# Wide mixing and moved routing products in layer 2, and a new order of all queues for the first two tiles, in a four-layer kernel on one core

## What is computed

```python
# layer 0: conditioning is a grouped convolution plus a bias per batch; ffn is base + LoRA of the best 2 of 28 experts
out = conv(x, weight) + (cond @ c_weight.T)[:, :, None] + bias[None, :, None]
y = out @ base_W.T + lora(out, top2(out @ gate_W.T))
# layers 1, 2, 3: conditioning mixes the 32 channels by a 32x32 table of each batch
h = gelu(gelu(cond @ W0 + b0) @ W1 + b1)
att = softmax(h @ W2 + b2)                                  # 64 x 8
agg_w = einsum('bk,koi->boi', att, weight)                   # 64 tables of 32 x 32
out = einsum('boi,bih->boh', agg_w, x) + (att @ bias_k)[:, :, None]
# ffn of layer 1: an 8-bit fake-quantised 512x512 product
# ffn of layer 2: (silu(out @ W_gate.T) * (out @ W_up.T)) @ W_down.T, 1792 hidden units
# ffn of layer 3: 2 of 3 experts for each batch, chosen by a router that looks at the first row's logits
#   and at the mean |out| of the first 9 channels and of the other 23
```

## Time and profile before

| | us |
|---|---|
| median of 3 runs | 780.34 |
| lowest, highest | 779.86, 783.27 |
| the profiled execution's own time | 779.9 |
| its span in the trace | 778.0 |
| PE busy | 750.6 (96%) |
| DVE, ACT, POOL busy | 478.1 (61%), 275.6 (35%), 419.5 (54%) |
| mean granted clock | 0.985 |

### The profile page before, as it was taken

How to read it: one execution, slowest core, us unless ns; L and a number is a source line. 1 busy time by engine, 2 the same in 40 slices (tenths; PEclk the granted TensorE clock), 3 DMA queues, 4 the chain that set the end, 5 groups by cost and what they waited for, 6 DMA issues and landing times.

```text
span 778.0 us, 11186 instructions
## 1 busy us (share of the span) xinstructions
PE 750.6 (96%) x3644; PEld 605.1 (78%) x3660; DVE 478.1 (61%) x1039; ACT 275.6 (35%) x532; POOL 419.5 (54%) x449
## 2 busy tenths in 40 slices
PE   8999999999899999999999999899899978999997
PEld 5587788787688888888788888777688766888886
DVE  2467667778623255753477256874788888576643
ACT  6444444453432233332424243232342332333211
POOL 2756667775425432111411045778677866778870
PEclk9699999999999999999999999999999998999999
DMA  9446446544051013100331022314313211212110
GB/s 281 71 109 168 160 154 199 164 136 136 28 190 54 28 59 91 55 29 1 94 109 20 10 73 81 131 56 135 124 42 117 60 41 56 69 42 83 55 41 27
DMA packets 49335, 69.60 MB, mean 89 GB/s; under 512 B 25864, under 2 KB 26120, under 8 KB 49016
## 3 DMA queue, kind: packets, MB, share of 16 engines
q1 hardware_dynamic: 39520, 38.65, 16.7%
q0 software_dynamic: 9152, 29.69, 12.5%
q10 hardware_dynamic: 608, 0.55, 0.2%
HBM read 45.71 MB, written 17.66 MB: 81 GB/s over the span
## 4 chain that ended last, share of the span: by engine, by line
PE 79%; DVE 14%; issue 3%; ACT 3%; DVEq 1%; ACTq 0%
PE bank L2024 23%; PE bank L1881 10%; PE bank L1975 9%; PE bank L2007 8%; PE bank L1720 8%; PE bank L1654 4%; PE bank L1758 3%; PE bank L1851 2%; DVE junk L1363 2%; PE bank L1790 1%; PE bank L1986 1%; PE bank L1770 1%; PE bank L1901 1%; DVE tl L1319 1%; ACT th L957 1%
## 5 line engine op out<-in xcount | busy, mean ns | idle before, releaser
L1512 DVE TENSOR_TENSOR sil<-bank,sil 128x512 f32<-128x512 f32 x56 | 38.6, 690 | 95.2 <-PE bank L2024 95.2
L1975 PE MATMUL bank<-wda,xch 128*128 (+1 forms) x272 | 87.9, 405 | 4.3 <-DVE xcl L1537 4.3
L2024 PE MATMUL bank<-th,wgr 128*128 128x512 f32 x224 | 88.3, 394 | 2.5 <-POOL tl L563 1.8
L1881 PE MATMUL bank<-wda,hh 128*128 128x512 f32 x224 | 88.4, 394 | 0.0
L2024 PE MATMUL bank<-th,wur 128*128 128x512 f32 x224 | 87.4, 390 | 0.0
L1881 PE MATMUL bank<-wda,hl 128*128 128x512 f32 x224 | 87.3, 390 | 0.0
L2024 PE MATMUL bank<-tl,wgr 128*128 128x512 f32 x224 | 87.2, 389 | 0.0
L2024 PE MATMUL bank<-tl,wur 128*128 128x512 f32 x224 | 87.2, 389 | 0.0
L1060 ACT ACTIVATE hh<-sil 128x512 fp32r<-128x512 f32 x56 | 35.4, 632 | 109.4 <-DVE sil L1512 109.4
L790 POOL TENSOR_TENSOR raw<-raw,bias 128x512 f32<-128x512 f32 x48 | 67.1, 1397 | 4.0
L1514 DVE TENSOR_TENSOR hl<-sil,hh 128x512 fp32r<-128x512 f32 x56 | 44.7, 798 | 39.1 <-ACT hh L1060 39.1
(11 more groups left out here) (329 smaller groups left out, 1880.4 us busy)
## 6 DMA issues: line engine op xcount, KB each, us to landing
tap<-in_x_taps_dram SPq DMA_DIRECT2D x16, 260.0 KB, 3.0
xin<-in_x_rows_dram SPq DMA_DIRECT2D x16, 256.0 KB, 3.0
xd<-xo SPq DMA_DIRECT2D x16, 256.0 KB, 3.2
xc<-xd SPq DMA_DIRECT2D x16, 256.0 KB, 3.3
xres<-xd SPq DMA_DIRECT2D x4, 1024.0 KB, 5.5
xd<-xres SPq DMA_DIRECT2D x4, 1024.0 KB, 4.7
tsd<-tf SPq DMA_DIRECT2D x4, 1024.0 KB
raw<-in_w_dram POOLq DMA_DIRECT2D x16, 256.0 KB, 3.1
```

What stands on the lines that cost most here:

```text
L1512: v.tensor_tensor(hf[:, m % 2], p_pre[(2 * m + 1) % 3][:], sil[:, m % 2], ALU.mult).then_inc(s_hf, 1)
L1881: last = mm(p_acc[j][:], h[:, m % HSLOTS, j * P:(j + 1) * P], wda[:, m * D:(m + 1) * D], start=(m == 0 and n == 0), stop=(m == MT - 1 and ...
L1975: last = mm(bank[(p + 1) % 2][:], x, y, start=(k == 0 and n == 0), stop=(k == KT - 1 and n == 2))
L2024: last = mm(p_pre[(2 * m + b) % 3][:], w[:, (m * KT + kt) * P:(m * KT + kt + 1) * P], x[:, kt], start=(kt == 0 and n == 0), stop=(kt == KT ...
```

## The change

**Tables.** The mix tables and biases come as one array of 64 x (3, 132), go through high and low parts (`mixh` on POOL, `mixl` on DVE), and three DMAs on POOL's queue (`stack_rows`) lay high, low and high rows over each other, 24 rows (`mix3`). `att3` holds the attention's high, high and low part side by side, 24 columns. `mixed(l)` is then one product with 24 rows for each of three banks, 396, 396 and 264 columns of split float32, with the bias in it.

**First two tiles.** PE: base(0) directly after conv(1), waiting for each quarter of the low weights; mixing_weights and mixed(0) after hidden(0), ahead of lora(0); mixed(1) after router(1); mixed(2) after conv(2); mix1(0) ahead of weights_t. POOL takes over `w0l`, DVE the second half of the weights' rounding (`weight_integers`). On POOL diag_tile(0), tap_lo(3) and diag_lo(0) follow each other. DVE does the softmax after gating(0) and `weight_scales` after t0_lo(1). ACT's order follows these.

**Boundaries of layer 2.** For groups 1 to 3 `cond2(c, j)` mixes tile j by three products of 512 columns ahead of down2 in m = 10..13, ACT adds the bias (`rows2_out`) into `tf`, and `features_t` transposes it with 16 float32 transposes between the groups; `t_hi_p` (ACT) and `t_lo_p` (DVE) take `th` and `tl` from PSUM. POOL's `t_lo`, DVE's `t_rows` and the bias broadcast stay for group 0 alone. x_hi and x_lo of tiles 2 and 3 move into m = 10..12.

**Routing products.** router_sums, class_rows, ranks(0) and permutation(0) stand behind down2(s, m-2) of their slice.

```diff
+            pool.wait_ge(d_mix, 16)
+            nc.gpsimd.tensor_scalar(mixh[:], mixr[:], 1.0, 1.0, ALU.mult, ALU.mult).then_inc(s_mix, 1)
+            pool.wait_ge(s_mix, 1)
+            stack_rows(0, mixh[:])
+            stack_rows(2, mixh[:])
+            pool.wait_ge(s_mix, 2)
+            stack_rows(1, mixl[:])
             tap_lo(1)
+            for k in range(KT):
+                pool.wait_ge(s_w0s, k + 1)
+                nc.gpsimd.tensor_tensor(w0l[:, k], w0_raw[:, k], w0h[:, k].bitcast(F32), ALU.subtract).then_inc(s_w0l, 1)
             pool.wait_ge(s_lbs, 1)
             nc.gpsimd.tensor_tensor(lbl[:], lb_raw[:], lbh[:].bitcast(F32), ALU.subtract).then_inc(s_lbs, 1)
-
-            def w1_integers(k):
-
-                pool.wait_ge(s_sw, 1)
+            tap_lo(2)
+            pool.wait_ge(s_sw, 1)
+            for k in range(KT):
                 nc.gpsimd.tensor_scalar(w1_raw[:, k], w1_raw[:, k], wsc[:, 2, k:k + 1], MAGIC, ALU.mult, ALU.add).then_inc(s_wqf, 1)
-                pool.wait_ge(s_wqf, k + 1)
-                nc.gpsimd.tensor_scalar(wq_rows[:, k], w1_raw[:, k], MAGIC, QMAX, ALU.subtract, ALU.min).then_inc(s_wqr, 1)
-
-            w1_integers(0)
-            w1_integers(1)
-            tap_lo(2)
-            w1_integers(2)
-            w1_integers(3)
+            x1_lo(0)
             diag_tile(0)
-            for t in range(1, TILES):
+            tap_lo(3)
+            diag_lo(0)
+            diag_tile(1)
+            x1_bias(0)
+            for t in range(2, TILES):
...
+                act.wait_ge(s_att, l + 2)
+                for src, c0, c1_ in ((bank[5], 0, 3), (bank[6], 3, 6), (bank[4], 6, 8)):
+                    nc.scalar.activation(aggs[:, l, c0 * MIXC:c1_ * MIXC], src[0:BATCH, 0:(c1_ - c0) * MIXC], ACT.Copy).then_inc(s_agc, 1)
...
+            def t_hi_p(c):
+                for kt in range(KT):
+                    act.wait_ge(s_tr2, (c - 1) * KT + kt + 1)
+                    nc.scalar.activation(th[:, kt], p_pre[kt][:], ACT.Copy).then_inc(s_th, 1)
+            def rows2_out(c, j):
+                act.wait_ge(s_cond, c * GT + j + 1)
+                if j == 0 and c == 1:
+                    act.wait_ge(s_tlp, 2)
+                    act.wait_ge(s_tld, 2)
+                    act.wait_ge(d_tab, 16 * 6 * BPT)
+                elif j == 0:
+                    act.wait_ge(d_tsd, 16 * (c - 1))
+                    act.wait_ge(s_lg, (c - 1) * GT)
+                nc.scalar.activation(tf[:, j], bank[3][:], ACT.Identity,
+                                     bias=bcol23[:, c * GT + j:c * GT + j + 1]).then_inc(s_te2, 1)
...
-            for t in range(TILES):
+            gate_exp(0)
+            act.wait_ge(d_lb, 16)
+            nc.scalar.activation(lbh[:], lb_raw[:], ACT.Copy).then_inc(s_lbs, 1)
+            conv_out(1)
+            act.wait_ge(s_at, 1)
+            nc.scalar.activation(atte[:], att[:], ACT.Exp).then_inc(s_g1, 1)
+            act.wait_ge(s_const, 9)
+            nc.scalar.activation(identb[:], ident[:], ACT.Copy).then_inc(s_constv, 1)
+            tap_hi(2)
+            t0_hi(1)
+            hidden_hi(0)
+            act.wait_ge(s_att, 1)
+            nc.scalar.activation(attt[:].rearrange("k l b -> k (l b)"), bank[5][0:3 * MIX, 0:COND_LAYERS * BATCH],
+                                 ACT.Copy).then_inc(s_atc, 1)
+            mixed(0)
+            mixed(1)
+            gate_exp(1)
+            x1_hi(0)
+            conv_out(2)
+            mixed(2)
+            tap_hi(3)
+            t0_hi(2)
+            hidden_hi(1)
+            diag_hi1(0)
+            mixed1(0)
+            for t in range(2, TILES):
                 step(t)
             x_hi(0, 2, 32)
             x_hi(0, 3, 32)
             integers_t(TILES - 2)
             x1_hi(TILES - 1)
             diag_hi1(TILES - 1)
-            t_hi(0)
+            t_hi()
             mixed1(TILES - 1)
...
                             ahead(s + 1)
                         else:
                             diag_hi(2 * LAST + 1)
+                    if s < LAST and m >= MT - GT:
+                        rows2_out(s + 1, m - (MT - GT))
+                        if m < MT - 2:
+                            x_hi(s + 1, m - (MT - GT) + 2, (s + 1) * 32 + 32)
                 if s < LAST:
-                    boundary(s + 1)
+                    t_hi_p(s + 1)
             def tokens_hi(t):
...
+            def mixing_softmax():
+                dve.wait_ge(s_m1, 2 * COND_LAYERS + 2)
...
+                dve.wait_ge(s_g1, 2 * COND_LAYERS + 1)
+                chain.link(v.tensor_reduce(attm[:, 1, :], atte[:], AX.X, ALU.add))
+                chain.link(v.reciprocal(attm[:, 2, :], attm[:, 1, :]))
+                chain.link(v.tensor_tensor(att[:], atte[:], rows(2), ALU.mult))
+                chain.link(v.tensor_copy(att3[:, :, 0], att[:]))
+                v.tensor_copy(att3[:, :, 1], att3[:, :, 0].bitcast(F32))
+                v.tensor_tensor(att3[:, :, 2], att[:], att3[:, :, 0].bitcast(F32), ALU.subtract).then_inc(s_at, 1)
...
+                if t == 0:
+                    mixing_softmax()
+                if t == 1:
+                    weight_integers()
                 hidden_lo(t)
                 if t + 1 < TILES:
                     t0_lo(t + 1)
+                if t == 0:
+                    weight_scales()
...
                         lo(1)
                 lo(3)
+            def t_lo_p(c):
+                for kt in range(KT):
+                    dve.wait_ge(s_th, c * KT + kt + 1)
+                    v.tensor_tensor(tl[:, kt], p_pre[kt][:], th[:, kt].bitcast(F32), ALU.subtract).then_inc(s_tld, 1)
             def residual(c, done, value):
                 dve.wait_ge(done, value)
...
                         order_one(0)
                     if s == LAST and m == 11:
                         indices(0)
+                    if s < LAST and MT - GT < m < MT - 1:
+                        x_lo(s + 1, (m - (MT - GT) + 1,))
                 if s < LAST:
-                    x_lo(s + 1)
-                    t_rows(s + 1)
+                    t_lo_p(s + 1)
                     residual(s, s_down, (s + 1) * MT)
...
-                    last = nc.tensor.transpose(bank[5][0:MIX, l * BATCH:(l + 1) * BATCH], att[:, l], ident[0:BATCH, 0:BATCH])
+                    last = nc.tensor.transpose(bank[5][0:3 * MIX, l * BATCH:(l + 1) * BATCH],
+                                               att3[:, l].rearrange("b r k -> b (r k)").bitcast(F32), ident[0:BATCH, 0:BATCH])
...
+            def mixed(l):
+                pe.wait_ge(d_mst, 48)
                 pe.wait_ge(s_atc, 1)
-                for l in range(COND_LAYERS):
-                    last = mm(bank[4][0:BATCH, 128 + l * CH:128 + (l + 1) * CH], attt[:, l], mixb[:, l], start=True, stop=True)
-                last.then_inc(s_mb, 1)
-
-            def mixed(l):
-
                 if l > 0:
                     pe.wait_ge(s_agc, 3 * l)
-                mm(bank[5][0:BATCH, :], attt[:, l], mixw[:, l, 0:512], start=True, stop=True)
-                mm(bank[6][0:BATCH, :], attt[:, l], mixw[:, l, 512:AGW], start=True, stop=True).then_inc(s_ag, 1)
-
-            def features(dst, weights, stop):
+                for dst, c0, c1_ in ((bank[5], 0, 3), (bank[6], 3, 6), (bank[4], 6, 8)):
+                    last = mm(dst[0:BATCH, 0:(c1_ - c0) * MIXC].rearrange("b (c n) -> b c n", n=MIXC), attt[:, l],
+                              mix3[:, c0:c1_, l], start=True, stop=True)
+                last.then_inc(s_att, 1)
...
                 router(t)
                 if t == 0:
                     scores()
+                if t == 1:
+                    mixed(1)
                 if t + 1 < TILES:
                     conv(t + 1)
-                if t == 0:
-                    mixing_weights()
-                    mixed(0)
+                if t == 1:
+                    mixed(2)
                 base(t)
-                if t == 0:
-                    mixed(1)
                 if t >= 2:
                     integers_t(t - 2)
                 if t + 1 < TILES:
                     positions(t + 1)
                 hidden(t)
                 if t == 0:
-                    mixed(2)
+                    mixing_weights()
+                    mixed(0)
+                if t >= 1:
+                    mix1(t - 1)
                 if t == 1:
                     weights_t()
-                if t >= 1:
-                    mix1(t - 1)
                 if t >= 2:
...
+            def cond2(c, j):
+                pe.wait_ge(s_gl, 2 * c)
+                if j < 2:
+                    pe.wait_ge(s_xclp, c * 2 + j + 1)
+                else:
+                    pe.wait_ge(s_xcld, c * 2 + j - 1)
+                if j:
+                    pe.wait_ge(s_te2, (c - 1) * GT + j)
+                elif c == 1:
+                    pe.wait_ge(s_tf, KT)
+                else:
+                    pe.wait_ge(s_clsd, c - 1)
```

(23 more changed lines are left out.)

187 lines of the change are left out of this document (77 added, 110 removed).

## The result

| | before | changed |
|---|---|---|
| median us (runs of the first comparison) | 780.34 (5) | 774.93 (5) |
| lowest, highest | 779.86, 783.27 | 773.79, 776.45 |
| profiled execution, span | 779.9, 778.0 | 775.81, 774.1 |
| ratio of the times, 95% interval | | 0.9922 [0.9897, 0.9946] |

The change makes the kernel 5.4 us faster, not 13.8. The direction held, the time lies 3.4 us above the range, and the gain is two fifths of the forecast.

The account below looks back on a forecast made before the run. PE was taken to bound the kernel, busy 750.6 of 778.0 us. Boundaries 4.9, routing 3.2 and front 5.1 sum to 13.2, off the profiled 779.9 giving 766.7, stated as 766.5; range 762.0 to 771.5.

Parts of the forecast that it names:

- Boundaries: Layer 2's three group boundaries: cheaper mixing and no stall give 1.64 us each, 4.9 in all; range 2.5 to 5.4.
- the stall: First gate products at each layer 2 boundary: the 0.61 us wait for DVE's and POOL's bias, high and low parts goes.
- Routing: Layer 2's last group: down2 put ahead covers PE's waits at router_sums and permutation; 3.2 us, range 1.9 to 3.8.
- Front: Layer 0's first tiles: router(2) 6.8 us earlier, less 1.7 for the clock, gives 5.1; range 3.0 to 7.5.
- router(0) ends at 16.1 as before: Start of the front walk: router(0) ends at 16.1 us, unchanged; conv(1) and base(0) follow.
- hm at 20.2, the softmax at 22.4: Front walk on DVE: gating takes 3.6 us from about 16.6, softmax follows, so mixed(0) runs 23.9 to 24.5.
- mix1(0) 2.2 behind the table: Front walk: table at POOL at about 35.3, then diag_tile 0.4, tap_lo(3) 1.3, low part 0.46; mix1(0) at 37.5.
- its own sign (mix1(0) after 39): Sign in the front: the forecast is wrong if mix1(0) starts after 39 us.
- a wait of 3.3 and the clock down behind it, 1.7: Front, ahead of mix1(0): PE newly waits about 3.3 us, and half clock behind it costs 1.7 us.
- router(2) as the place that counts: Front: tile follows tile from router(2), so its move from 47.60 to 40.8, 6.8 us, is the gain before clock loss.
- the third: Rival: boundary chain stalls and routing waits return at DVE's pace; boundaries 1, routing 1.9, front 3: 774 us; chance 0.08.
- The front gives less: Rival: each late step of the table's chain delays mix1(0) one for one; front 1 to 2, 769 to 771 us; chance 0.20.

Follow-up runs that it names:

- the wide mixing alone: Kernel before with only the wide mixing at layer 2's three boundaries; front and routing as before: 777.94 us, ratio 0.9996.
- the front alone: Kernel before with only the changed kernel's tables and queues for tiles 0 and 1; boundaries and routing as before: 786.39 us, ratio 1.0077.
- the mended front: Changed kernel with low parts on DVE, tap 4's load then scales' store directly behind the table loads, and ACT, POOL and PE steps reordered: 764.30 us, ratio 0.9800.
- POOL's silence: Changed kernel with layer 0's and LoRA weights' low parts on DVE, tap 2's low part held until attention is transposed: 773.05 us, ratio 0.9938.

## Why the prediction was wrong

**Boundaries: right.** 4.9 was forecast and 5.2 measured, in the changed kernel and in the wide mixing alone. At the boundary shown the transposes were 1.67 and not 1.90; the stall went, and ACT's `tf` wasn't waited for. The Trainium skill's figure that spoke against this (page "TensorE: Matmul & The Clock Gate", section "Wait — 56ns, not 53.3ns?") is 55.6 ns at 128 columns; the transposes took 1.67/16 = 0.104 us each, so here too the measurement decides against it.

**Routing: right in size, with a hidden condition.** 3.2 forecast, 3.4 measured, and the gather became the end of the group, as forecast. What wasn't seen is that the waits are worth more than their length: the front alone and the wide mixing alone lost 2.9 and 4.1 us in the last group by the clock, and the forecast had read from one execution that 2.2 us are harmless.

**Front: 5.1 forecast, a loss of 3.9 measured.** Two steps failed, hm and the softmax, and router(2) taken as the end. The terms of the 9.0 between are: 1.4 for the late start, 3.7 more up to mixed(0) (28.99 against 23.9), 1.2 from there to mix1(0) (14.8 against 13.6), 0.2 won from there to router(2), 4.6 behind router(2), less the 1.7 that the forecast had already taken off for the clock. By the steps of that walk:
- *router(0) ends at 16.1 as before.* It began 1.43 later. The 20 products without use at the start took longer (to 8.6 us instead of 7.2), and they do so in kernels with before's front too: router(0) was at 15.6 to 15.8 in three of those runs, and at 14.5 to 14.6 in two runs with a changed front. So this goes with the execution, and nothing shows the change to cause it. Counted from router(0), the way to group 0 took 183.99 before and 186.49 in the changed kernel, so of the 3.9 the change has 2.5.
- *hm at 20.2, the softmax at 22.4.* This is the first step that failed. It took gating(0) as 3.6 us from a row of before in which POOL ran too, but the 5 us of w0l on POOL, which the walk itself had just placed there, weren't laid over it. hm came at 25.00 and the attention at 27.95, 3.4 and 4.1 beyond the late start. The runs price it: in the mended front, low parts on POOL instead of DVE cost 4.25 us by group 0; in the changed kernel POOL's silence moved router(2) by 2.0 only, for the reasons given there.
- *mix1(0) 2.2 behind the table.* It was 3.4 behind (40.38 to 43.82), because ACT's bd1h stood behind t0_hi(2) and hidden_hi(1), and POOL's low part waited 0.92 for it. The table's own way, 9.6 forecast, took 9.1 (31.31 to 40.38). By its own sign (mix1(0) after 39) the forecast was wrong here. The rows, POOL's and ACT's:

```profile
40.38 0.52 POOL L504 TENSOR_TENSOR bd1f<-ag,mask 128x128 f32<-128x128 f32 x1 [1.43 <-DMA bcol<-aggd]
...
42.61 0.38 ACT L924 ACTIVATE hts<-bank 112x256 fp32r<-112x256 f32 x1
42.87 0.31 ACT L904 ACTIVATE bd1h<-bd1f 128x128 fp32r<-128x128 f32 x1
```

- *a wait of 3.3 and the clock down behind it, 1.7.* The wait was 1.5, since PE was late as well; the clock fell instead behind the 4.6 us ahead of mixed(0), and stood at 0.50 in 28 to 34. Of the 6.3 us that the clock was to give back, about 3.5 came, an estimate: 33.1 us at a mean clock of 0.79 before, 31.1 at 0.89 in the changed kernel, each us at half clock taken as half a us lost.
- *router(2) as the place that counts.* This is the second step that failed, and the larger one. The forecast ended there. The moved store of the scales and the load of tap 4 behind it on SP weren't priced at all; they cost 3.03 and 1.4 of clock one tile later, and the run with tap 4 moved gave 4.4 of it back.

One slip in the sum besides: 13.2 off the median is 767.1, and the forecast took it off the profiled 779.9 and rounded down to 766.5.

The rival that came nearest was the third, 774 us by a partly used front and waits of DVE, but its reason was wrong: neither boundaries nor routing fell short. "The front gives less" had the mechanism, one chain in which each late step counts one for one, and a price that was too small by 5 to 6.

## What to carry to other kernels

When a step moves from one engine to another, lay its new place over what the engine next to it does at that time: a long POOL instruction held five of DVE's small ones, in a serial chain, for what was left of it. When a queue gets a new order, price every instruction of it up to where the old rhythm is back, DMAs included, and ask what stands behind a wait and behind a slow transfer. And a wait of PE of 2 us is not always worth 2 us: behind two of 2.2 and 2.3 the clock stayed up, and behind two of 2.5 and 2.6 it fell and cost 4.1 more, which filling them with products without use gave back.

## What the runs showed that wasn't expected

- DVE operations of 1 to 28 columns took 0.97 to 2.30 us beside POOL's subtractions of 512 to 1024 columns, 0.15 to 0.30 without them, and each ended within 0.05 us of a POOL instruction's end.
- A store of 512 single values took about 10 us from issue to landing (40.78 to 50.76), and table loads that were put behind it on the same queue arrived 5.7 us later.
- In the last group half clock came behind waits of 1.88, 2.51 and twice 2.56 us and not behind two of 2.22 and 2.27. The mean clock of before over 61 executions went with its time, from 770.65 us at 0.993 to 785.18 at 0.976. Which wait is followed by half clock in a given execution stays open.
- Twenty useless products of 512 columns in the last group made a kernel 5 us faster (777.94 to 772.96).
